# One pass instead of two for the neighbourhood scores of tiles 4 to 15, with stacked operands spread by 32 more DMAs

## The reference

```
qkv = (layernorm(x) @ qkv_w + qkv_b)           # 4 heads of 16
attn = einsum(q / 4, keys of the 7x7 window) + bias(relative position)
out = softmax(attn) @ values of the window     # then projection, residual
x = x + out;  x = x + mlp(layernorm(x))
t = t + global_attention(layernorm(t))         # 8 heads over 1024 tokens
t = t + routed_ffn(layernorm(t))               # a scan of 33 steps that picks weights
```

## Time and profile before

| what | us |
|---|---|
| median of 3 runs | 572.45 (571.07 to 573.36) |
| profiled execution | 576.68 |
| its span, first to last instruction | 574.9 |
| TensorE busy | 496.4 (86%) |
| VectorE busy | 391.2 (68%) |
| ScalarE busy | 294.8 (51%) |
| GpSimd busy | 57.0 (10%) |

### The profile page before, as it was taken

One profiled execution on the slowest core, in us unless ns is written; L12 is line 12 of the kernel. 1 busy time (PEld: TensorE's weight loads), 2 busy tenths in 40 slices (PEclk: granted clock), 3 DMA queues, 4 the chain that ended last, 5 costly groups with the idle time before them and its releaser, 6 DMA issues.

```text
span 574.9 us, 12552 instructions
## 1 busy us (share of the span) xinstructions
PE 496.4 (86%) x5103; PEld 250.9 (44%) x5104; DVE 391.2 (68%) x722; ACT 294.8 (51%) x443; POOL 57.0 (10%) x108
## 2 busy tenths in 40 slices
PE   5888889775899899999999999999999563699872
PEld 5565666541334354444444444444443221376621
DVE  5885777579666558768966877667652355898762
ACT  1765466651365745565555554565546244665441
POOL 8252143131100000100000010000000100000000
PEclk9999998997699999999999999999999956999976
DMA  4201000000000000000000000000000000000001
GB/s 113 46 2 38 1 3 0 2 20 1 1 1 1 1 2 2 1 20 2 1 2 1 2 2 1 2 2 1 1 2 1 11 3 16 1 1 1 1 0 38
DMA packets 10224, 5.01 MB, mean 9 GB/s; under 512 B 9012, under 2 KB 9271, under 8 KB 10167
## 3 DMA queue, kind: packets, MB, share of 16 engines
q1 hardware_dynamic: 8886, 4.19, 3.1%
q10 hardware_dynamic: 1281, 0.01, 0.1%
HBM read 2.09 MB, written 0.52 MB: 5 GB/s over the span
## 4 chain that ended last, share of the span: by engine, by line
PE 65%; DVE 16%; issue 9%; ACT 5%; POOL 2%; DMA 1%; SPq 1%; DVEq 0%; ACTq 0%; POOLq 0%
PE PS L797 17%; PE PS L773 17%; PE PS L757 6%; DVE most L1591 4%; PE PS L813 3%; PE PS L531 2%; PE PS L1021 2%; PE PS L503 2%; PE PS L515 2%; PE PS L688 2%; PE PS L700 2%; DVE sbias L1637 2%; PE PS L714 1%; PE PS L604 1%; ACT PT L1219 1%
## 5 line engine op out<-in xcount | busy, mean ns | idle before, releaser
L1591 DVE TENSOR_REDUCE most<-PS 128x2 f32<-128x1024 f32 x128 | 156.1, 1222 | 83.2 <-PE PS L757 82.4
L1219 ACT ACTIVATE PT<-PS 128x1024 f32<-128x1024 f32 x128 | 124.6, 1021 | 118.9 <-PE PS L773 118.8
L773 PE MATMUL PS<-qS,aS 64*64 64x512 f16 x1024 | 124.7, 383 | 1.8 <-ACT PT L1219 1.6
L773 PE MATMUL PS<-qS,kS 64*64 64x512 f16 x1024 | 124.3, 383 | 0.0
L797 PE MATMUL PS<-PT,V 128*64 128x512 f32 x512 | 121.8, 596 | 0.0
L773 PEld LDWEIGHTS PS<-qS,kS 64*64 64x64 f16 x1024 | 58.6, 109 | 25.8 <-issue 2.0
L773 PEld LDWEIGHTS PS<-qS,aS 64*64 64x64 f16 x1024 | 58.6, 109 | 25.6 <-ACT PT L1219 4.6
L757 PE MATMUL PS<-aS,qS 64*64 64x512 f16 x256 | 52.5, 403 | 11.2 <-DVE most L1591 10.4
L797 PEld LDWEIGHTS PS<-PT,V 128*64 128x64 f32 x512 | 34.0, 137 | 46.4 <-issue 41.9
L1176 ACT ACTIVATE prob<-sbias,negm 128x320 f32<-128x320 f32 (+1 forms) x64 | 34.3, 538 | 35.9 <-DVE negm L1637 35.3
L757 PE MATMUL PS<-kS,qS 64*64 64x512 f16 x256 | 52.4, 403 | 0.0
(11 more groups left out here) (199 smaller groups left out, 692.0 us busy)
## 6 DMA issues: line engine op xcount, KB each, us to landing
xall<-in_x_dram SPq DMA_DIRECT2D x2, 256.0 KB, 4.4
qS<-kS SPq DMA_DIRECT2D x4, 128.0 KB, 2.9
q0M<-kS SPq DMA_DIRECT2D x4, 128.0 KB, 2.4
kS<-aS SPq DMA_DIRECT2D x4, 128.0 KB, 2.3
out_dram<-x SPq DMA_DIRECT2D x4, 128.0 KB, 2.1
w<-in_L_attn_Wq_dram SPq DMA_DIRECT2D x2, 128.0 KB, 2.6
w<-in_L_attn_Wk_dram SPq DMA_DIRECT2D x2, 128.0 KB, 2.7
w<-in_L_attn_Wv_dram SPq DMA_DIRECT2D x2, 128.0 KB, 2.6
```

The costliest lines, as they stand in the source:

```text
L773: mm = pe.matmul(PS[h0:h0 + C, score_banks(t) + lane, :], input_of(lane, k_part)[:, k0 + h0:k0 + h0 + C], qS[C * lane:C * lane + C, q_part ...
L1219: act.activation(PT[:, g % 2, :, phase, :], PS[:, b0:b0 + 2, :], ACT.Exp).then_inc(c1["exped"], 1)
L1591: dve.tensor_reduce(most[:, g % 2, u // 2, u % 2, :], PS[:, try_bank(a):try_bank(a) + 2, :], AX.X, ALU.max, negate=True)\
```

## The change

Tiles 0 to 3 (u = 0 to 15) keep the two passes. For tiles 4 to 15 (u = 16 to 63) the two planes of queries are stacked in rows instead: head h has 64 rows, 32 with the high query part and 32 with the low one, and the keys are copied so that the same 32 rows of `k0S` stand beside both. Two heads then fill the 128 rows, so the keys come in two pairs, `k0P[h // 2]`, and the queries of the other head of the pair stay zero. One pass gives what two gave. `qS` now holds the two-pass queries of tiles 0 to 3 (`q0F`), the stacked queries of tiles 4 to 7 (`q0L`) and the stacked keys of image 0 (`k0P0`); `q0M1` is half as large, and `k0P1` is new.

```diff
-                for part in range(2):
-                    mm = pe.matmul(PS[:, u % 2, 0:rows * WW], q0M[img][:, h, part, t * P:(t + 1) * P],
-                                   k0S[:, img, first * WW:(first + rows) * WW],
-                                   start=(part == 0), stop=(part == 1))
+                if T in (FEW, NT) and h == 0:
+                    pe.wait_ge(heads_stacked[img], 16 * 4 * NH0)
+                keys = slice(first * WW, (first + rows) * WW)
+                if T < FEW:
+                    for part in range(2):
+                        mm = pe.matmul(PS[:, u % 2, 0:rows * WW], q0F[:, h, part, t * P:(t + 1) * P], k0S[:, 0, keys],
+                                       start=(part == 0), stop=(part == 1))
+                else:
+                    queries = q0L[:, h, t * P - BLK:(t + 1) * P - BLK] if img == 0 else q0M1[:, h, t * P:(t + 1) * P]
+                    mm = pe.matmul(PS[:, u % 2, 0:rows * WW], queries, (k0P0, k0P1)[img][:, h // 2, keys],
+                                   start=True, stop=True)
...
-            for img in range(B):
-                if img:
-                    power(2)
-                link(pool.memset(q0M[img][:, :, :, :].rearrange("p h l t -> p (h l t)").bitcast(F32), 0.0))
-                pool.sem_inc(heads_cleared, 1)
+            link(pool.memset(q0F[:, :, :, :].rearrange("p h l t -> p (h l t)").bitcast(F32), 0.0))
+            pool.sem_inc(heads_cleared, 1)
+            power(2)
+            link(pool.memset(q0L[:, :, :].rearrange("p h t -> p (h t)").bitcast(F32), 0.0))
+            pool.sem_inc(heads_cleared, 1)
+            link(pool.memset(q0M1[:, :, :].rearrange("p h t -> p (h t)").bitcast(F32), 0.0))
+            pool.sem_inc(heads_cleared, 1)
...
+            def stack_heads(img, queries, keys, toks):
+
+                sp.wait_ge(heads_cleared, img + 2)
+                for part in range(2):
+                    for h in range(NH0):
+                        hr, row = slice(32 * h, 32 * h + 32), 64 * (h % 2) + 32 * part
+                        sp.dma_start(queries[row:row + 32, h, :], q0S[hr, img, part, toks]).then_inc(heads_stacked[img], 16)
+                side_wait(sp, ("k", img, 1))
+                for part in range(2):
+                    for h in range(NH0):
+                        hr, row = slice(32 * h, 32 * h + 32), 64 * (h % 2) + 32 * part
+                        sp.dma_start(keys[row:row + 32, h // 2, :], k0S[hr, img, :]).then_inc(heads_stacked[img], 16)
+
+            stack_heads(0, q0L, k0P0, slice(BLK, TOK))
+            side_wait(sp, ("q", 1, 1))
+            stack_heads(1, q0M1, k0P1, slice(0, TOK))
```

More of the change, by code:

```diff
@@ L166, in build @@
         xb = sb("xb", [P, B * NT, C])
-        q0M1 = sb("q0M1", [P, NH0, 2, TOK], F16)
+        q0M1 = sb("q0M1", [P, NH0, TOK], F16)
+        k0P1 = sb("k0P1", [P, 2, TOK], F16)
         k0S = sb("k0S", [P, B, TOK], F16)
@@ L195, in build @@
         q0S = kS[:, :, :].rearrange("p i (n t) -> p i n t", n=2)
-        q0M = [qS[:, :, :, :].rearrange("p a l (n t) -> p (a l) n t", n=2), q0M1]
+        qSrow = qS[:, :, :, :].rearrange("p a l t -> p (a l t)")
+        q0F = qSrow[:, 0:NH0 * TOK].rearrange("p (h i t) -> p h i t", h=NH0, i=2)
+        q0L = qSrow[:, NH0 * TOK:NH0 * (TOK + BLK)].rearrange("p (h t) -> p h t", h=NH0)
+        k0P0 = qSrow[:, NH0 * (TOK + BLK):NH0 * 2 * TOK].rearrange("p (n t) -> p n t", n=2)
         weight = sb("weight", [P, 2, QT, 2])
@@ L283, in build @@
         heads_spread = [sem(f"nat_heads_spread_{img}") for img in range(B)]
+        heads_stacked = [sem(f"nat_heads_stacked_{img}") for img in range(B)]
         ln_chain = sem("ln_chain")
@@ L389, in build @@
         LN1_STEP = 1
+        FEW = NT // 2
         SUM_STEP = 39
@@ L682, in nat_score @@
                     pe.wait_ge(c0["biased"], u - 1)
[L683 to L686, removed]
-                for part in range(2):
-                    mm = pe.matmul(PS[:, u % 2, 0:rows * WW], q0M[img][:, h, part, t * P:(t + 1) * P],
-                                   k0S[:, img, first * WW:(first + rows) * WW],
-                                   start=(part == 0), stop=(part == 1))
+                if u == 0:
+                    side_wait(pe, ("k", 0, 0))
+                    side_wait(pe, ("k", 0, 1))
+                    pe.wait_ge(heads_spread[0], 16 * NH0)
+                if T in (FEW, NT) and h == 0:
[9 more added lines that the diff above has]
+                                   start=True, stop=True)
                 mm.then_inc(c0["scored"], 1)
@@ L1937, in _ @@
                   .then_inc(weights_loaded, 16)
[L1939 to L1944, removed]
+            sp.wait_ge(heads_cleared, 1)
+            side_wait(sp, ("q", 0, 1))
+            for h in range(NH0):
+                hr = slice(32 * h, 32 * h + 32)
+                sp.dma_start(q0F[hr, h, :, :], q0S[hr, 0, :, 0:BLK]).then_inc(heads_spread[0], 16)
+            def stack_heads(img, queries, keys, toks):
[6 more added lines that the diff above has]
+                for part in range(2):
+                    for h in range(NH0):
+                        hr, row = slice(32 * h, 32 * h + 32), 64 * (h % 2) + 32 * part
[3 more added lines that the diff above has]
+            stack_heads(1, q0M1, k0P1, slice(0, TOK))
             for img in range(B):
```

## The result

The changed kernel took 579.08 us (median of six runs, 575.40 to 580.43 and one of 590.44); the kernel before took 572.52 in the same comparison (571.07 to 573.36). The ratio (not the quotient of the two medians) is 1.0099, 95% interval 1.0072 to 1.0127: slower by 1%, and the median lies 2.7 us beyond the upper end of the range. The profiled execution of before had taken 576.68, 4.2 us over its median; that of after took 578.76, near its own. So the two traces differ by only 2.0 us of span (574.9 and 576.9), and the remaining 4.6 us of the loss have to be looked for in the runs, not in this pair of traces.

A forecast was written before the change was run, and what follows sets the result against it. It took TensorE and VectorE to hand work to each other, neither pacing the neighbourhood stage alone. Terms -0.8 - 2.4 + 1.9 + 1.3 = 0.0 gave 572.4 us against the median 572.45; range 569.0 to 576.4.

The forecast's parts named there:

- The pass that goes: Scores of units 16 to 63: 48 matmuls fewer, of which those on the chain gain 2.4 us, bounds 1.3 to 3.0.
- The shorter first clearing: At the start, GpSimd's halved clearing of qS frees VectorE's first bias-table copy sooner: gain 0.8 us, bounds 0.6 and 0.95.
- The 32 more DMAs: At unit 16, TensorE waits for sixteen copies that SP issues one by one: loss 1.9 us, from none to 4.1.
- rival B: SP as slow as on large copies: stall at unit 16 3.4 to 4.1, longer slow clock, say 576 us; chance 0.22.
- The clock: Behind unit 16's wait, one stretch of TensorE at half clock: loss 1.3 us, bounds 0 and 2.6.
- Rival C: TensorE's thinner work between 109.6 and 119.8 us lets its clock fall once more: at most 1 us, 573.4; chance 0.08.

The follow-up runs named there:

- e1: The kernel before with one pass in image 1 alone; image 0 keeps two passes, its old copies and the old first clearing; 573.94 us, ratio 1.0028.
- e4: The kernel before with GpSimd's first clearing cut into two halves, nothing else; 572.46 us, ratio 0.9990.
- e3: Keys first twice: the changed kernel with image 0's key copies issued before its query copies and the one pass repeated in units 16 to 63; 572.28 us.
- e2: Keys first: the changed kernel with image 0's eight key copies issued before its eight query copies; 573.90 us, ratio 0.9999.
- f1: The changed kernel timed again without any edit; 581.85 us (579.00 by the counted runs), ratio 1.0103.
- e5: The changed kernel with its one pass done twice, the copies and the wait at unit 16 kept; 579.16 us, ratio 1.0095.
- f2: Keys first with one pass (e2) timed again without any edit; 574.65 us, ratio 1.0014.
- e6: Keys first (e2) with the pass done twice in image 1 only, one pass in tiles 4 to 7 of image 0; 569.99 us, ratio 0.9945.

## Why the prediction was wrong, step by step

**The pass that goes: right.** 2.4 us were taken; keys first against keys first twice shows 2.2 from unit 16 to unit 63 (78.16 - 75.93) and 2.5 at equal clock (mean of 569.7 and 570.1 against 572.4).

**The shorter first clearing: right in kind, its size not settled.** Taken 0.8, bounds 0.6 and 0.95. From the row of `xn` to the first `sbias` it took 16.60 us before and 15.38 after, 1.2. Against e1, which has the old clearing and one copy of the queries that took 1.09 us, it is 1.0 (16.35, first `sbias` at 26.58). Against e4, which clears as much as before and had no slow copy, it is only 0.4 (15.74). At equal clock e3 is 0.8 faster than before, and e4 0.5. So against a start without a slow copy the gain is 0.4, and the rest is that a slow copy no longer delays the first `sbias`: e2 has one of 1.39 us, and 15.38 all the same.

**The 32 more DMAs: mis-sized, 1.9 for 3.8 us.** (There are 36 where there were 8, so 28 more on balance.) The step that failed is the price of one copy. From one copy to the next I took 0.50 for 32 KB, between the 0.46 of the `pw` loads and the 0.64 of the large copies, and 0.60 for 64 KB; it was 0.63 for both, 0.59 of it to issue. That is 1.25 of the 1.9 us that were missed. One copy that took 1.54 makes 0.95 more, and a landing after 2.0 instead of 2.3 gives 0.3 back. The traces of f1 and e5 have a late copy among these sixteen too, and TensorE starts at 47.44 and 47.51. Seen from 35.05, fifteen of these (9.4), the one late copy (0.9), 2.0 to land and 0.14 make 47.5, where 47.63 was measured. That is rival B's mechanism, and the stall is within its 3.4 to 4.1. The Trainium skill, page "DMA: Bandwidth & Descriptors", section "Rules for kernel authors", says to join small transfers, since under 64 KB one pays mostly overhead; the trace agrees, by the 0.62 us for 32 KB and for 64 KB alike. That a copy of 32 KB costs SP as much as one of 128 KB was the prediction's own step from there, and the 0.59 us to issue either bears it out. The 4 KB loads of `pw` were the wrong row to lean on; the right one was the row with the same kind of transfer, from SBUF to SBUF. Whether the `pw` loads were cheaper by their size or by their source no run shows.

**The clock: the step that failed most, 1.3 for about 6 us.** The sum priced only the half clock behind the wait; for the thinner work it had nothing. The changed kernel loses 38.4 and 40.8 us to the clock and before 26.7; 0.49 x 11.7 to 14.1 is 5.7 to 6.9. Two parts of it were seen apart. Behind the wait: e5 loses 31.4 and e3 26.8, which is 2.2 us; I had taken 1.3 for it, and rival B 1.7 to 2.6. From the thinner work: keys first loses 33.2 and 34.5, which is 3.2 to 3.8 us without any wait. They add up to 5.4 to 6.0. These are estimates by the common slope, and with the scatter of the clocks each is uncertain by about 1 us.

**Rival C: its mechanism was right, its price was not.** I looked at 109.6 to 119.8, forecast 5.9 us of busy time there and found 5.95 in e2, at full clock. "VectorE paces there, so it costs at most 1" asked only about that stretch. In the trace of after the longest stretch of half clock lies at the stage's end, where TensorE scores for the global attention: the chain of waits from 126 to 158 us, by line, begins

```profile
by line: DVE most L1606 36.3%; PE PS L786 19.9%; PE PS L770 13.6%; PE PS L727 8.1%; PE PS L744 6.2%; PE PS L713 4.1%; PE PS L736 2.7%; DVE qS L1599 1.9%; DVE mean L1461 1.8%; PE PS L810 1.8%; DVE yh L1565 1.3%; issue 1.1%; DVE most L1708 0.
```

and TensorE's own lines in it make 56%. From unit 63 to the first `head_outputs` it took 48.4 to 48.8 us where half clock lasted 10.2 to 10.3 (e4, f2, e6), 50.3 with 17.1 (before) and 52.3 with 30.7 (after). So half clock there is paid for in the next stage. It is not the only place: in f1's trace unit 16 to unit 63 took 9.75 us longer than before. C's condition was also too narrow: it asked for the work of one stretch, and the runs show the lowest clock with less work in both images. B and C stood as alternatives, at 576 and 573.4; the result is both at once.

**The sum redone** with what was measured: -1.0 - 2.3 + 3.8 + 6 = +6.5, against 6.6 (579.08 - 572.52). The parts come from different kernels, and the first of them may be as small as 0.4, so that they meet so closely is partly luck.

**The base.** I noted that the profiled execution lay 4.2 us above the median, and then treated its stretches of half clock as those of the kernel. They were those of an unlucky run: mean clock 0.946, where the median run of before has 0.954. e2's profiled run was, the other way round, a lucky one. One trace shows which stretches can come, not how often.

**What stays open.** Why thinner work lets the clock fall longer is not shown, only that it does: e2 and e3 differ in nothing but 48 repeated matmuls. Nor is it shown where the clock falls in the slower runs of keys first, 574 to 577 us, since both of its traces (e2, f2) are of faster ones. The 3.8 us and the half clock behind the wait were not taken apart further, for instance by a wait of half the length.

## What to carry to other kernels

Where TensorE hands work to and fro with another engine, a matmul saved is not only its own time: it also thins out the work, and the clock may take back as much as was saved or more (here 3.2 to 3.8 us for 2.2 to 2.5). So time the leaner kernel with its passes repeated as well; if the repeated one is no slower, keep the repetition at the places where it is off the chain and the lean form where it is on it (here image 0 lean and image 1, or only its last 16 units, repeated). Price many small DMAs of one queue by the row of the same kind of transfer (here 32 to 128 KB cost SP the same), and issue first those whose data is ready first: changing the order of two groups of eight removed a 3.8 us wait. And where the profiled run is not near the median, compare the mean clocks of all runs before believing a difference of two traces.

## What the runs showed of the hardware

SP needed 0.59 us to issue a copy from SBUF to SBUF, with 32, 64 and 128 KB alike, and now and then one of 1.1 to 1.9 us (1.54 here, 1.39 and 1.53 in e2, 1.35 before, 1.09 and 1.65 in e1, 1.87 in e3). GpSimd's clearing held up VectorE's copy by its whole rest: 2.96 us for the copy with a clearing of 3.5, 1.23 with one of 1.8; cut in two it held up two copies (e4). The mean clock of runs of one kernel on one chip went from 0.931 to 0.955 (f2), 7.0 us from the fastest run to the slowest, and the kernel with more matmuls had the narrower spread (e3: 0.945 to 0.959, 4.8 us).
